# A 16-batch hybrid network on one core: the first mixture's results collected inside the next norm, and its down weights split by Pool

## The reference, cut to what matters

```
x = x + four layers of (mamba, norm, attention, norm, gelu network)(norm(x))
x = x + ffn(norm(x))            # the first mixture, n = 0
x = x + sparse_attention(norm(x))
x = x + ffn(norm(x))            # the second mixture, n = 1
...
ffn(x): shared = silu(x @ w1) * (x @ w2) @ w3            # hidden width 512
        two of 16 experts for each token, by sigmoid(x @ router_w) + bias
        out = shared + sum of gate * swiglu_expert(x)     # expert width 128
```

## Time and profile before

| | us |
|---|---|
| median of 3 runs | 2846.8 |
| lowest, highest | 2831.41, 2847.91 |
| the profiled execution | 2852.53 |
| its span, first to last instruction | 2850.8 |
| TensorE busy | 2327.4 (82%) |
| VectorE busy | 1686.2 (59%) |
| ScalarE busy | 1645.8 (58%) |
| Pool busy | 700.1 (25%) |

### The profile page before, as it was taken

The page is one execution under the profiler, slowest core; times in us unless marked ns, Lnnn a source line. Parts: engine busy times, 40 slices in busy tenths (PEclk is TensorE's granted clock), DMA queues, the critical chain, the costliest instruction groups (busy, mean ns, idle before and its releaser), DMA issues.

```text
span 2850.8 us, 54378 instructions
## 1 busy us (share of the span) xinstructions
PE 2327.4 (82%) x16356; PEld 1476.7 (52%) x16356; DVE 1686.2 (59%) x2866; ACT 1645.8 (58%) x2539; POOL 700.1 (25%) x976
## 2 busy tenths in 40 slices
PE   6978889977888987888997888969756699996885
PEld 4544445644444644444564444546654477764575
DVE  4567753657773556774465777356323678865642
ACT  6447775636776645777554777655432156665452
POOL 0123210012221012231002232117563100002754
PEclk8969989978999996999997999989877799998997
DMA  2033310023330013331003332041321233324133
GB/s 108 20 102 92 113 47 6 8 76 93 110 92 7 9 32 99 104 102 36 14 0 91 100 102 79 7 82 50 113 72 36 74 94 98 97 59 85 51 115 124
DMA packets 137819, 199.42 MB, mean 70 GB/s; under 512 B 15681, under 2 KB 91969, under 8 KB 137409
## 3 DMA queue, kind: packets, MB, share of 16 engines
q1 hardware_dynamic: 128448, 178.45, 21.9%
q0 software_dynamic: 9216, 19.02, 1.8%
HBM read 98.04 MB, written 96.76 MB: 68 GB/s over the span
## 4 chain that ended last, share of the span: by engine, by line
PE 50%; issue 12%; DVE 11%; POOL 10%; DMA 9%; ACT 5%; SPq 2%; DVEq 1%; POOLq 1%; ACTq 0%
PE ps L1047 7%; PE ps L1072 6%; POOL back_scratch L2566 5%; POOL slot_scratch L2561 5%; DVE hmx L2095 4%; PE ps L853 4%; DMA hqk<-hmt 3%; PE ps L816 2%; PE ps L780 2%; DMA hqk<-hqk_scratch 2%; PE ps L786 2%; PE ps L892 2%; DMA hqk_scratch<-hqks 2%; PE ps L731 2%; PE ps L928 2%
## 5 line engine op out<-in xcount | busy, mean ns | idle before, releaser
L2095 DVE TENSOR_REDUCE hmx<-ps 128x2 f32<-128x512 f32 x768 | 506.8, 688 | 222.8 <-PE ps L1047 218.5
L1635 ACT ACTIVATE hpt<-ps 128x1024 f32<-128x1024 f32 x512 | 519.9, 1020 | 61.9 <-PE ps L1059 61.0
L1047 PE MATMUL ps<-hqk 24*128 24x256 f32 x2048 | 307.3, 359 | 153.3 <-DVE hmx L2095 99.4
L1047 PEld LDWEIGHTS ps<-hqk 24*128 24x128 f32 x2048 | 197.3, 208 | 366.6 <-DVE hmx L2095 255.1
L1072 PE MATMUL ps<-hpt,hvx 128*32 128x256 f32 x4096 | 304.1, 419 | 15.9 <-ACT hpt L1635 15.4
L1059 PE MATMUL ps<-hqk 26*128 26x256 f32 x2048 | 273.8, 349 | 2.4 <-ACT hpt L1635 1.6
L1656 ACT ACTIVATE hrow<-ps 128x512 f32<-128x512 f32 x256 | 151.9, 593 | 203.0 <-PE ps L1047 203.0
L2103 DVE TENSOR_REDUCE hmx<-hrow 128x2 f32<-128x512 f32 x256 | 176.0, 687 | 45.2 <-ACT hrow L1656 35.9
L1059 PEld LDWEIGHTS ps<-hqk 26*128 26x128 f32 x2048 | 163.4, 198 | 23.9 <-ACT hpt L1635 18.4
L2566 POOL DMA_INDIRECT back_scratch<-ys,xslot x160 | 153.2, 958 | 86.6 <-issue 47.9
L2003 DVE TENSOR_REDUCE mxs<-ps 128x2 f32<-128x512 f32 x256 | 164.0, 680 | 14.8 <-PE ps L892 13.6
(11 more groups left out here) (299 smaller groups left out, 5243.5 us busy)
## 6 DMA issues: line engine op xcount, KB each, us to landing
hqk_scratch<-hqks SPq DMA_DIRECT2D x64, 768.0 KB, 3.2
hqk<-hqk_scratch SPq DMA_DIRECT2D x256, 192.0 KB
qk_scratch<-qks SPq DMA_DIRECT2D x16, 768.0 KB, 3.3
slot_scratch<-filler SPq DMA_DIRECT2D x10, 1040.0 KB, 15.9
xslot<-slot_scratch SPq DMA_DIRECT2D x20, 520.0 KB
yback<-back_scratch SPq DMA_DIRECT2D x32, 256.0 KB, 4.5
k<-qk_scratch SPq DMA_DIRECT2D x16, 384.0 KB
qv<-qk_scratch SPq DMA_DIRECT2D x64, 96.0 KB
```

The lines of the kernel that those rows point to most:

```text
L1047: return mm(ps[:, o % 2, qt * SEQ:(qt + 1) * SEQ], hqk[r][32 * g:32 * g + 24, j, 0, qt * P:(qt + 1) * P], hqk[r][32 * g:32 * g + 24, j, 1, ...
L1635: A(hpt[:, j, g:g + 2, :, :], ps[:, 2 + g:4 + g, :], ACT.Exp, scale=QSCALE).then_inc(hd_exp, 1)
L2095: V.tensor_reduce(hmx[:, r, :, 4 * g + j], ps[:, o % 2, :].rearrange("p (t k) -> p t k", t=2), AX.X, ALU.max).then_inc(hd_max[o % 2], 1)
```

## The change

- Gate STAGE_A is removed. SP starts the mixture without it; VectorE and Pool wait instead for the last chunk of the fourth layer's network (`f_out`), Pool also for its own `win_set`.
- Pool makes `w3h` itself, right behind its tables, and then `w3l`; ScalarE's copy is removed. This holds for both mixtures.
- Gate EXP_F1 is removed. In the first mixture TensorE collects chunk c + 1 ahead of the centring of chunk c of norm 10, in banks 6 and 7 in turn, and the centring waits for VectorE's addition. VectorE makes the additions of chunks 0 to 2 ahead of its first multiplication of the norm, and each later one behind the multiplication that stands before it. Pool clears when the last chunk has been collected by TensorE.
- In the second mixture the collection stays behind the mixture, now in banks 6 and 7 too.

```diff
@@ SP @@
-            passed(sp, STAGE_A)
             experts(0)
@@ PE @@
-            def collect(n):
-
-                for c in range(NC):
-                    pe.wait_ge(chunk_in[c], 16 + 32 * (n + 1))
-                    for t in range(4):
-                        for part in range(2):
-                            last = mm(ps[:, c, t * P:(t + 1) * P], yback[:, c, part, t, :], ident[:], start=part == 0,
-                                      stop=part == 1)
-                    last.then_inc(e_t, 1)
+            def collect(n, c):
+
+                pe.wait_ge(chunk_in[c], 16 + 32 * (n + 1))
+                pe.wait_ge(e_out, nth(e_out, routed_out(n, max(c - 2, -1))))
+                for t in range(4):
+                    for part in range(2):
+                        last = mm(ps[:, 6 + c % 2, t * P:(t + 1) * P], yback[:, c, part, t, :], ident[:], start=part == 0,
+                                  stop=part == 1)
+                last.then_inc(e_t, 1)
+
+            def collected(c):
+
+                if c == 0:
+                    collect(0, 0)
+                if c < NC - 1:
+                    collect(0, c + 1)
+                pe.wait_ge(e_out, nth(e_out, routed_out(0, c)))
...
-            gate(pe, STAGE_A)
             pe.wait_ge(load_g, 32)
...
             experts(0)
-            gate(pe, EXP_F1)
-            norm(10, res)
+            norm(10, res, ready=collected, hooks={"apart": None})
             gate(pe, LN_B)
...
             experts(1)
+            for c in range(NC):
+                collect(1, c)
@@ ACT @@
-                A(w3h[:], G("w3"), ACT.Copy).then_inc(act_step, 1)
...
-            gate(act, STAGE_A)
...
-            gate(act, EXP_F1)
@@ DVE @@
-                for c in range(NC):
+
+            def collect(n, *chunks):
+
+                for c in chunks:
                     dve.wait_ge(e_t, nth(e_t, turned(n, c, back=True)))
-                    V.tensor_tensor(res[:, c * CH:(c + 1) * CH], ps[:, c, :], res[:, c * CH:(c + 1) * CH], ALU.add)\
+                    V.tensor_tensor(res[:, c * CH:(c + 1) * CH], ps[:, 6 + c % 2, :], res[:, c * CH:(c + 1) * CH], ALU.add)\
                         .then_inc(e_out, 1)
...
-            gate(dve, STAGE_A)
+            dve.wait_ge(f_out, every(f_out, LAYERS * NC - 1))
             norm(9, xa, added=True)
             dve.wait_ge(load_g, 32)
             experts(0)
-            gate(dve, EXP_F1)
-            norm(10, xa)
+            norm(10, xa, hooks={("before", 0, 0): lambda: collect(0, 0, 1, 2), ("before", 0, 1): lambda: collect(0, 3),
+                                ("before", 0, 2): lambda: collect(0, 4), ("before", 0, 3): lambda: collect(0, 5),
+                                ("before", 1, 0): lambda: collect(0, 6), ("before", 1, 1): lambda: collect(0, 7)})
...
             experts(1)
+            collect(1, *range(NC))
@@ POOL @@
                 tables(n)
-                pool.wait_ge(act_step, act_steps[n] + 1)
+                pool.wait_ge(load_g, 32)
+                G_.tensor_copy(w3h[:], G("w3")).then_inc(w3_high, 1)
+                pool.wait_ge(w3_high, n + 1)
                 G_.tensor_tensor(w3l[:], G("w3"), w3h[:].bitcast(F32), ALU.subtract).then_inc(w3_set, 1)
...
-            gate(pool, STAGE_A)
+            pool.wait_ge(win_set, LAYERS + 1)
+            pool.wait_ge(f_out, every(f_out, LAYERS * NC - 1))
             experts(0)
-            gate(pool, EXP_F1)
+            pool.wait_ge(e_t, nth(e_t, turned(0, NC - 1, back=True)))
             clear_queries()
             clear_operands(cleared(LAYERS - 1))
             gate(pool, LN_B)
```

## The result

| | before | after |
|---|---|---|
| median, us | 2847.4 (6 runs) | 2864.1 (6 runs) |
| lowest, highest, us | 2831.4, 2853.3 | 2855.2, 2870.4 |
| ratio after / before, 95% interval | | 1.0061, 1.0040 to 1.0083 |
| the profiled execution, its span | 2852.5, 2850.8 | 2861.6, 2859.9 |
| TensorE / VectorE / Pool busy | 2327.4 / 1686.2 / 700.1 | 2322.5 / 1689.1 / 705.3 |

What follows compares the result with a forecast made beforehand. No engine was taken to bound the whole, so each edit was priced in its own stretch: -0.1 - 3.4 + 4.3 + 8.0 = +8.8 us, from the median of 2846.8 to 2855.6, with a range of 2838 to 2866.

Steps and rivals of the forecast that it cites:

- the favoured case: The forecast's own mechanism for the whole kernel, +8.8 us to 2855.6, range 2852 to 2860, chance 0.48.
- the wide range: Whole time from 2838 to 2866 us, taking in all but most of the lost clock and half of the paying case.
- The gate before norm 9: Replacing the gate before the ninth norm by a wait on f_out saves 0.1 us; bounds 0 and -0.46.
- The scans: VectorE's routing scans, freed from Pool's subtraction, take 1.22 us: -1.4 in the first mixture, -2.0 in the second, -3.4 together.
- Pool between the additions: Before norm 9, Pool's copy and subtraction get in among VectorE's eight additions, delaying the first multiplication: +4.3 us.
- addition 8 ahead: Rival before norm 9: VectorE's eighth addition gets in ahead of Pool's subtraction; sum +4.8 us, 2851.6, chance 0.17.
- is busy for 17.36 of 18 us: Step at norm 9: TensorE, busy from 1877 to 1895, has no idle time to take up the +4.3 us.
- TensorE loses its clock: Rival in the interleaved collection and norm 10: waits drop TensorE to half clock, 12.3 us more, 2868, chance 0.13.
- The clears behind the last collected chunk: Gate behind norm 10 waits for Pool's 16.4 us of clears, now started after the last collected chunk: +8.0 us.
- interleaving pays: Rival at norm 10: the gate doesn't wait for Pool, so the stretch gains 2.8 us; whole -6.0, 2840.8, chance 0.07.
- the walk: Step-by-step timing of TensorE's and VectorE's queues in norm 10: last chunk collected at 2162.0, last multiplication ending at 2174.1.

Runs made afterwards that it cites:

- split alone: Kernel before with only Pool casting, then subtracting the down weights right behind its tables, ScalarE's copy gone: one run, 3031.4 us beside 3031.1.
- late split on the kernel before: Kernel before with Pool casting and subtracting the down weights, in the first mixture only behind VectorE's eighth addition: 2841.8 us beside 2848.2, ratio 0.9970.
- early drain: Changed kernel plus a drain of Pool right behind the first mixture's last indirect DMA: ratio to the kernel before 1.0022, and 1.0049 when repeated.
- two drains: Changed kernel plus Pool drains behind the first mixture's last indirect DMA and between its 64 slot DMAs and the 80 sending results back: one run, 3042.8 us.
- clears early: Changed kernel plus a Pool drain behind the last indirect DMA, ten of twelve clears moved ahead of the wait for the last collected chunk: 2857.5 us beside 2848.2.
- additions first: Changed kernel plus a Pool drain behind the last indirect DMA, VectorE making four additions before norm 10's first multiplication, later ones a step sooner: 2861.2 us beside 2848.2.
- split late: Changed kernel with Pool's cast and subtraction in the first mixture held until VectorE's eighth addition: ratio to the kernel before 1.0029, and 1.0041 when repeated.
- all together: Changed kernel with Pool's drain early, first-mixture split behind the eighth addition, ten clears moved ahead and additions a step sooner: 2840.7 us beside 2848.2, ratio 0.9970.

## Why the prediction was right, and where it was short

The sign, the range and the mechanisms that were priced came out. But the forecast was short by 8 us through two terms that it does not have, its own range for the favoured case (2852 to 2860) was missed, and the time lies 2 us inside the upper end of the wide range, which had been opened for other rivals; that it is inside owes something to luck.

**The gate before norm 9, -0.1.** Right: 0.46 to 0.35 us between the write and the additions.

**The scans, -1.4 and -2.0.** Right: both L2196 scans took 1.22 us in the changed kernel. The stage D to E fell by 4.4, though; in the twelve executions with the split moved it lies between 446.0 and 448.9, and two kernels with the same code in that stage (split alone, and late split on the kernel before) are 2.9 us apart. So the one profile of before (451.6) may be 2 us on the long side. That isn't settled.

**Pool between the additions, +4.3.** Right in mechanism and size. The cast took 2.37 (2.4 forecast) and came while VectorE was in its additions; it held the seventh, and the subtraction the eighth. The two took 8.79 us together, the seventh 2.80 (2.9 forecast) and the eighth 6.07 (6.1 forecast: 1877.66 to 1883.75). The first multiplication came 4.15 us later, or 4.3 without the 0.1 of the gate. The rival, addition 8 ahead, fell. The Trainium skill (SBUF — State Buffer, section SBUF: two separate sides) describes such a pair as an exclusive lock that is held for the whole instruction; the trace agrees, with the eighth addition ending 0.54 us behind Pool's subtraction, and 5.00 us for all eight as soon as Pool stays out.

**The step that failed in this stage** is the sentence that TensorE "is busy for 17.36 of 18 us, so that no idle time takes up the delay". It asked only whether idle time could absorb the delay, and not what the delay does to TensorE: it had to stand still until VectorE came, for 6.13 us, and went on at half its clock. The same text shows the clock at 0.50 behind a pause of 23.5 us and names "TensorE loses its clock" as a rival, but only for the interleaved stretch. It cost 4.7 us here. First multiplication to scan took 36.1 to 36.6 us in the eight executions with stretched additions and the pause (the changed kernel twice, early drain twice, two drains, split alone, clears early, additions first) and 31.3 to 31.4 in the five without (before, split late twice, all together, the kernel before with a late split). The gate makes no difference to it, since it stands in kernels of both groups. The edits move Pool's two instructions, so they add or remove the pause only together with the meeting on VectorE; that Pool's work beside TensorE doesn't itself lower the clock is seen in the late splits, where the two instructions run beside the norm at a granted clock of 1.00.

**The clears behind the last collected chunk, +8.0.** Right as far as it went. The last chunk was done 27.2 us behind C (27.4 forecast), TensorE waited 1.32 and 3.10 us for additions behind multiplications (1.7 and 3.5 forecast), the last multiplication ended before the clears, and with the drain paid early the stage is +7.9. The rival "interleaving pays" fell with it. Two sums of the walk do not come out of its own terms: V3 ends at 2154.3 by them and not at 2154.9, and the last multiplication at 2173.3 and not at 2174.1. The first made no odds, since TensorE pauses 0.41 us there for ScalarE's square, which the walk leaves out.

**A rival that came true in part, and at no cost,** is "TensorE loses its clock in the interleaved stretch" (0.13). In the wait of 3.10 us the granted clock fell to 0.50 and stayed there from 31.1 to 37.9 us behind C, and the last multiplication ended 40.8 us behind C (39.3 by the walk). Of the eight executions with this wait, the clock fell in five; in the other three (two drains, split late and early drain, once each) the last multiplication ended 38.7 to 38.8 behind C. These 2 us are hidden: the clears ended 2.8 us later still (4 to 5 forecast).

**The term that was missing** is the gate's own drain of Pool, 6.60 us, which makes +14.4 of +8.0. The prediction put 0.1 us between the end of the clears (2178.7) and the load of the indices (2178.8), about what it is in the kernel before between the last instruction that the gate waits for and that load. But Pool's drain there was short only because the gate EXP_F1, which the change removes, had drained Pool's queue of the same indirect DMAs 32 us earlier under cover. The removed gate was priced for its waits (its pause ahead of the norm) and for what it released (the clears), not for what its drain did.

**The sum.** Forecast -0.1 - 3.4 + 4.3 + 8.0 = 8.8. Measured: -0.1 - 3.4 + 4.3 + 4.7 + 14.4, and -2.4 unexplained in D to E: 17.4 by stages (17.5 by these rounded terms), 16.8 in the medians. The two missing terms, 4.7 and 6.6, are together more than the miss; the D to E stage gave part of it back.

## What to carry to other kernels

When a gate or drain is removed, ask what it had already finished for the next one: its price can be small only because it is paid under cover, and the next drain on the same engine inherits it. When a delay is put in front of TensorE, price it twice, once as the delay and once as the stretch at half clock that may follow if TensorE stands still for it (here 4.3 to 6.1 us); whether idle time takes up the delay is only half the question. And an engine's side work that reads SBUF belongs behind a row of VectorE's two-operand instructions, not in it: moved behind the eighth addition, the same two instructions of Pool turned a loss of 7.4 us in the stage into a gain of 1.7 to 3.5. Of these 1.7 is like with like, since the profile of before has the fallen clock at the start of norm 9 too; the rest is that clock's chance.

## What the runs showed of the hardware that was not expected

- Pool's first drain behind indirect DMAs costs about 6.6 us from the later of two times, the end of the last one or the drain's own turn: 6.62, 6.58 and 6.61 us right behind the last of them, and still 6.60 when it came 49 us later with memsets between. The drain of the gate behind the second mixture, in the kernels before and after alike, also ended 6.61 us behind its last indirect DMA. A drain after that costs 0.04, or as long as clears still under way take (7.03). It is the same for 80 DMAs and for 144; behind the 64 slot DMAs alone it was 5.3. What it waits for isn't settled.
- In pauses of TensorE of 4.3, 4.4 and 6.1 us at the start of norm 9 the granted clock fell to 0.50 of 2.4 GHz each time, for 10.3 us in the changed kernel (1874.9 to 1885.2), at a cost of 4.7 to 5.3 us (36.1 to 36.6 against 31.3 to 31.4).
- Shorter pauses cost the clock in some executions and not in others, at the same place of the same code. Behind the pause of 2.0 to 2.3 us ahead of the first centring of norm 9 it was 0.50 for 3.4 us in eight of thirteen executions, the profile of before among them; in the wait of 3.1 us in norm 10 it fell to 0.50 in five of eight, for 6.8 us in four of them and 3.4 in the fifth.
- On some chips the stages of indirect DMAs are much longer with the same kernel: from the first slot DMA to the last that sends results back 289 to 297 us in place of 204 to 205, and from the second mixture's first slot DMA to its first collected chunk 296 to 302 in place of 208 to 211. Those two differences make up the 180 us or so by which the kernel before takes longer there. Why isn't settled.
